# Cross attention over 257 keys: chunks of 128 + 128 + 1 in place of three chunks of 86

## The reference

```
qh = (q @ Wq.T).reshape(B, Tq, H, hd).transpose(0, 2, 1, 3)
kh = (k @ Wk.T).reshape(B, Tk, H, hd).transpose(0, 2, 1, 3)
vh = (v @ Wv.T).reshape(B, Tk, H, hd).transpose(0, 2, 1, 3)
...
scores = jnp.einsum('bhqd,bhkd->bhqk', qh, kh) / np.sqrt(hd)
scores = scores + attn_mask
scores = jnp.where(key_padding_mask[:, None, None, :], NEG_INF, scores)
attn = jax.nn.softmax(scores, axis=-1)
out = jnp.einsum('bhqk,bhkd->bhqd', attn, vh)
...
return out @ Wo.T
```

## Time and profile before

| | |
|---|---|
| time, median of 3 runs (lowest to highest) | 2710.31 us (2709.35 to 2710.75) |
| profiled execution | 2713.56 us |
| its span, first to last instruction | 2711.9 us |
| mean granted TensorE clock | 0.925 |
| busy share of the span: PE, PEld, DVE, ACT, POOL | 84%, 63%, 62%, 50%, 41% |
| the loop of this stage, PE busy in 600 us of it | 595.87 us |
| the same, DVE, ACT, POOL | 465.06, 426.63, 331.55 us |

### The profile page before, as it was taken

One profiled execution on the slowest core, in us unless ns is written; L12 is line 12 of the kernel. 1 busy time (PEld: TensorE's weight loads), 2 busy tenths in 40 slices (PEclk: granted clock), 3 DMA queues, 4 the chain that ended last, 5 costly groups with the idle time before them and its releaser, 6 DMA issues. The chain is left out here.

```text
span 2711.9 us, 91330 instructions
## 1 busy us (share of the span) xinstructions
PE 2288.5 (84%) x32292; PEld 1709.6 (63%) x32293; DVE 1673.4 (62%) x4691; ACT 1360.2 (50%) x3761; POOL 1123.8 (41%) x1094
## 2 busy tenths in 40 slices
PE   6968888883999949996999999999788888649990
PEld 3646666662788736774777777777555555536670
DVE  3556666665677653333777777777578888643341
ACT  2544444442677523332777777777555556412330
POOL 0013333331677510003555555555166666475114
PEclk9989999995999759997999999999899999859995
DMA  4610000000000000001111001100000000022112
GB/s 125 175 46 1 0 0 0 0 0 3 2 0 0 1 28 5 0 0 37 32 30 39 29 29 35 34 29 29 29 2 0 0 0 0 1 96 80 37 37 66
DMA packets 34605, 71.67 MB, mean 26 GB/s; under 512 B 6864, under 2 KB 22224, under 8 KB 33744
## 3 DMA queue, kind: packets, MB, share of 16 engines
q1 hardware_dynamic: 29904, 60.99, 7.6%
q0 software_dynamic: 4608, 9.45, 1.1%
HBM read 60.98 MB, written 9.44 MB: 26 GB/s over the span
## 5 line engine op out<-in xcount | busy, mean ns | idle before, releaser
L2529 DVE CUSTOM_DVE_ANT_0 xat_scores<-bank,xat_mask_b 128x257 f32<-128x257 f32 x512 | 212.8, 423 | 100.9 <-PE bank L2247 92.2
L2401 ACT ACTIVATE xat_scores<-xat_scores,xat_least 128x257 f32<-128x257 f32 x512 | 257.4, 503 | 15.0 <-DVE xat_least L2529 14.9
L2304 PE MATMUL bank<-ident,xat_scores 128*86 128x128 f32 x1536 | 241.0, 280 | 0.0
L2304 PEld LDWEIGHTS bank<-ident,xat_scores 128*86 128x86 f32 x1536 | 158.0, 122 | 83.5 <-ACT xat_scores L2401 40.9
L989 POOL TENSOR_TENSOR gqa_rnorm<-gqa_norm_min,gqa_minus_half 128x12 f32<-128x12 f32 x64 | 145.8, 2278 | 126.7 <-DVE gqa_norm_min L1058 126.7
L2415 ACT ACTIVATE xat_p_T<-bank 86x384 f32<-86x384 f32 x256 | 122.6, 479 | 121.9 <-PE bank L2304 121.9
L624 POOL TENSOR_TENSOR lin_k_exp<-lin_k_exp,lin_k_rsum 128x512 f32<-128x512 f32 x64 | 67.0, 1047 | 266.4 <-DVE lin_k_rsum L662 261.8
L1707 DVE SCALAR_TENSOR_TENSOR X<-bank,expert_shares,X 128x128 f32 (+1 forms) x256 | 72.2, 344 | 156.6 <-PE bank L1670 156.4
L1399 POOL TENSOR_TENSOR bat_scores<-bat_scores,bat_max 128x512 f32<-128x512 f32 x128 | 131.7, 1040 | 56.0 <-DVE bat_max L1432 55.0
L1693 ACT ACTIVATE moe_gelu<-bank 128x512 f32<-128x512 f32 x128 | 76.4, 597 | 153.5 <-PE bank L1662 153.5
L1670 PEld LDWEIGHTS bank<-moe_w,moe_gelu 128*128 128x128 f32 x1024 | 124.2, 192 | 30.1 <-issue 18.7
(11 more groups left out here) (301 smaller groups left out, 6359.7 us busy)
## 6 DMA issues: line engine op xcount, KB each, us to landing
glu_ctx_N<-in_ctxN SPq DMA_DIRECT2D x32, 576.0 KB, 4.4
xat_ctx_T<-in_ctxT SPq DMA_DIRECT2D x32, 516.0 KB, 3.5
expert_w<-in_glx_w SPq DMA_DIRECT2D x3, 2048.0 KB, 15.7
xat_pad<-in_xat_pad SPq DMA_DIRECT2D x32, 128.5 KB, 3.4
slot_rows<-glx_zero POOLq DMA_DIRECT2D x40, 64.0 KB, 10.5
slt_rows<-slot_rows SPq DMA_DIRECT2D x40, 64.0 KB, 1.8
slot_results<-slt_y POOLq DMA_DIRECT2D x40, 64.0 KB, 1.8
moe_w<-in_moe_w SPq DMA_DIRECT2D x2, 1024.0 KB, 5.8
```

What stands on the lines that cost most here:

```text
L2304: m = pe.transpose(dst[0:JC, c * P:(c + 1) * P], sx[j % 2][g][:, c * JC:(c + 1) * JC], k.ident[:, :])
L2401: act.activation(sx[j % 2][g][:, 0:J], sx[j % 2][g][:, 0:J], ACT.Exp, bias=mn[j % 2][g][:, 0:1], scale=-1.0, accum_out=sm[j % 2][:, g:g + ...
L2529: dve.tensor_tensor_reduce(sx[j % 2][g][:, 0:J], pS[g][:, 0:J], mb[slot][:, j, :], 1.0, BIG, ALU.add, ALU.min, mn[j % 2][g][:, 0:1]).then_ ...
```

## The change

`v` and the turned exponentials are kept with 128 keys on the partitions for each of the first two chunks. The last key (number 256) is handled apart, in small products:

- `p_transpose`: two transposes of 128 x 128 for each group in place of three of 128 x 86. With group 3, four products (form 128*32) of the last score column, repeated 32 times, with the identity bring the last key of each of the four groups into 32 partitions of the same bank; the copy of group 3 is 384 columns wide as before, those of groups 0 to 2 are 256 wide.
- `v`: two products of 128 keys in place of three of 86, and four products of 32 columns (form 128*32, 32 moving columns) for the last key. Its copy is 288 columns in place of 384.
- `o`: eight products with 128 rows in place of twelve with 86, and four with one active row, at partitions 0, 32, 64 and 96, for the last key, added to the same results.

No wait, no order of the parts and no other function is changed.

```diff
+    FULL = J // P
+    LAST = J - 1
+    width = [FULL * P] * (G - 1) + [FULL * P + P]
...
-        va = [sb(f"v{i}", [JC, NJ, P]) for i in range(2)]
+        va = [sb(f"v{i}", [P, 2 * P + 32]) for i in range(2)]
...
-        pt = [[sb(f"p_T{i}_{g}", [JC, NJ * P]) for g in range(G)] for i in range(2)]
+        pt = [[sb(f"p_T{i}_{g}", [P, width[g]]) for g in range(G)] for i in range(2)]
...
-                for c in range(NJ):
+                for c in range(FULL):
                     for g in range(G):
                         r = slice(32 * g, 32 * g + 32)
-                        m = pe.matmul(dst[r, OC], va[j % 2][:, c, r], pt[j % 2][g][:, c * P:(c + 1) * P],
-                                      start=(c == 0), stop=(c == NJ - 1))
+                        pe.matmul(dst[r, OC], va[j % 2][:, c * P + 32 * g:c * P + 32 * g + 32],
+                                  pt[j % 2][g][:, c * P:(c + 1) * P], start=(c == 0), stop=False)
+                for g in range(G):
+                    one_row = slice(32 * g, 32 * g + 1)
+                    m = pe.matmul(dst[32 * g:32 * g + 32, OC], va[j % 2][one_row, FULL * P:FULL * P + 32],
+                                  pt[j % 2][G - 1][one_row, FULL * P:FULL * P + P], start=False, stop=True)
                 m.then_inc(no_made, 1)
...
-                for c in range(NJ):
-                    m = pe.matmul(dst[0:JC, c * P:(c + 1) * P], cT[slot][:, j, c * JC:(c + 1) * JC], wv[:, :],
+                for c in range(FULL):
+                    pe.matmul(dst[:, c * P:(c + 1) * P], cT[slot][:, j, c * P:(c + 1) * P], wv[:, :],
+                              start=True, stop=True)
+                for g in range(G):
+                    m = pe.matmul(dst[32 * g:32 * g + 32, FULL * P:FULL * P + 32],
+                                  cT[slot][:, j, LAST:LAST + 1].broadcast_to([P, 32]), wv[:, 32 * g:32 * g + 32],
                                   start=True, stop=True)
...
-                for c in range(NJ):
-                    m = pe.transpose(dst[0:JC, c * P:(c + 1) * P], sx[j % 2][g][:, c * JC:(c + 1) * JC], k.ident[:, :])
+                for c in range(FULL):
+                    m = pe.transpose(dst[:, c * P:(c + 1) * P], sx[j % 2][g][:, c * P:(c + 1) * P], k.ident[:, :])
+                if g == G - 1:
+                    for i in range(G):
+                        m = pe.matmul(dst[32 * i:32 * i + 32, FULL * P:FULL * P + P],
+                                      sx[j % 2][i][:, LAST:LAST + 1].broadcast_to([P, 32]), k.ident[:, :],
+                                      start=True, stop=True)
...
-                act.activation(va[j % 2][:, :, :], unit_bank(*at)[0:JC, 0:NJ * P].rearrange("p (c f) -> p c f", f=P),
-                               ACT.Copy).then_inc(v_copied, 1)
+                act.activation(va[j % 2][:, :], unit_bank(*at)[:, 0:FULL * P + 32], ACT.Copy).then_inc(v_copied, 1)
...
-                act.activation(pt[j % 2][g][:, :], unit_bank(*at)[0:JC, 0:NJ * P], ACT.Copy).then_inc(pa_copied, 1)
+                act.activation(pt[j % 2][g][:, :], unit_bank(*at)[:, 0:width[g]], ACT.Copy).then_inc(pa_copied, 1)
...
-                dve.tensor_copy(pt[j % 2][g][:, :], unit_bank(*at)[0:JC, 0:NJ * P]).then_inc(pd_copied, 1)
+                dve.tensor_copy(pt[j % 2][g][:, :], unit_bank(*at)[:, 0:width[g]]).then_inc(pd_copied, 1)
```

## The result

| | before | changed |
|---|---|---|
| median of 4 runs (lowest to highest) | 2710.53 us (2709.35 to 2714.51) | 2753.39 us (2746.52 to 2763.76) |
| profiled execution | 2713.56 us | 2757.49 us |
| its span | 2711.9 us | 2755.7 us |

The changed kernel is slower: ratio 1.0159, 95% interval 1.0122 to 1.0196, or +43 us in the medians and +44 us in the profiled executions. The forecast was 2748 us, 1.4% slower, with a range of 2729 to 2760. A second set of runs of both gave 1.0172 (1.0135 to 1.0209).

What follows compares the result with a forecast made beforehand. TensorE's own program was taken as the bound. Fewer full records against more changes of form gave +0.36 us a step, +46 us for 128 steps, less 8 us of waits: +38, so 2748 us, 1.4% slower, range 2729 to 2760.

Steps and rivals of the forecast that it cites:

- TensorE's own program is the bound: In the loop TensorE is busy 595.87 of 600 us, with a small wait in some steps.
- Fewer full records: Transposes of groups 0 and 1 lose two records, -0.20 us a step; group 2 loses one, -0.11.
- The change inside `o`: In `o`, the new change from 32 columns x 128 rows to 32 x 32: +0.15 us a step.
- Group 3: Group 3's transposes with the last key's small products: from 0.36 to 0.73 us, +0.37 a step.
- `v` and what follows it: `v`'s full and small products and the next group's new start: mean +0.17 us a step.
- The sum: All terms of a step together: +0.38 us, taken as 0.36, or +46 us for 128 steps.
- The waits of step 0 and 1: TensorE's waits before the scores, 0.18 us in step j = 0 and 0.06 in j = 1, go: -8 us.
- Copies cost and bring nothing: Shorter copies on VectorE and ScalarE only lengthen their idle time as long as TensorE is the bound.
- no price inside `o`: Rival: the change from 128-row to 32 x 32 form in `o` is free, 19 us less, 2729 us; 8%.
- only with a wait: Rival: a change of form costs only where TensorE also waits for a semaphore; 2705 us, 0.2% faster; 5%.
- products of one row don't share the array: Rival: `o`'s four one-row products run one behind the other, +0.65 us a step, 2832 us; 3%.
- Free changes, faster: Rival: changes of form overlap with the records around them; if free, -46 us, 2664 us; 4%.

Runs made afterwards that it cites:

- keep_later: `last_behind_o` with VectorE's `o_keep` moved behind `least` of group 3: 2728.92 us, 0.9944 of the kernel before.
- o_all_rows: Changed kernel with `o`'s four last-key products taking all 128 rows instead of one (output not the reference's): 2737.31 us, 18 us under the changed kernel.
- v_last_first: Changed kernel with `v`'s four small products put ahead of its two full ones: 2719.28 us, 1.0048 of the kernel before.
- spread_apart: Kernel before with the four products spreading the reciprocals moved out of `o`, between keys and group 2's transposes: 2776.00 us, 1.0120 of the kernel before.
- last_behind_o: Changed kernel with the last key's small products of group 3 and `v` both directly behind `o`: 2695.77 us, 0.9957 of the kernel before.

## Why the prediction was right, and what was mis-sized

The direction, the mechanism and the time held; 38 us were forecast, 43 to 44 measured. The 5 us between are one term that was too small and a rounding the wrong way, less smaller errors against them. The terms hold one by one, group by group of the table; only in the last few us is the nearness owed to errors that cancel.

- *TensorE's own program is the bound.* Right before, and more so after: 599.98 of 600 us.
- *Fewer full records.* -0.20 and -0.11 forecast, -0.21 and -0.11 read.
- *The change inside `o`*, bounded by nothing and 0.15 and taken as 0.15: 0.13, shown by the all-rows kernel.
- *Group 3*: +0.37 forecast and read.
- *`v` and what follows it*: the term that was too small. I had 0.055 us for the slow start of full products with 128 weight columns, from L809. That is a transpose, one pass. `v`, the queries and the output projection are two-pass products (two records each), and after a change they start 0.10 late: the output projection has 1.09 - 0.98 = 0.11 more. `v` itself has the 0.05 too, in every step, but its small products were priced 0.02 too dear, so the table shows less. In the mean of the four steps the term is 0.22 us where I had 0.17, 6 us in 128 steps.
- *The sum*: worked out it was 0.38, and I took 0.36. That rounding added 2 to 3 us to the shortfall. `o`'s 0.15 for 0.13 took about as much back. The steps grew by 0.07, 0.40, 0.47 and 0.46 us, and with the 0.24 of waiting that went, TensorE's own work grew by 1.64 / 4 = 0.41 a step: 52 us, less the 8 of the waits 44.
- *The waits of step 0 and 1*, 8 us, vanish: step j = 0 grew from 4.96 to 5.03 us in the mean, against 0.47 and 0.46 in j = 2 and 3. The trace's list of waits has none of TensorE for `least` any more, where the earlier trace rows had 54. Right, and `keep_later` shows the chain at work, in the kernel with both sets behind `o`.
- *Copies cost and bring nothing*: VectorE's copy of 256 columns takes 414 ns for 546, ScalarE's 374 for 479, and all of it went into idle time.

Of the rivals, "no price inside `o`" falls by the timeline and by `o_all_rows`; "only with a wait" by `v_last_first`, where moving products that had no wait ahead of them gave 36 us; "products of one row don't share the array" by the timeline after, where eight one-row records take 0.35 us to the next group and eight 128-row records 0.36; the clock stayed at 1.00. "Free changes, faster" was wrong in its premise, and of its 46 us (1.7%) the best order that keeps the output gives 0.44%: two of the new changes stand in it still. The rule of the Trainium skill, TensorEngine Tiling (Array Packing), section Key Properties, that a change of tiling mode drains the engine, agrees with `spread_apart`: 0.27 us for two changes. The overhead of about 60 cycles a matmul that the same page of the Trainium skill gives (section Instruction Overhead) does not fit here if it is charged to each record in turn: by the prediction's estimate from it `v`'s eight small records would take 0.2 us by themselves. They take 0.19 us with the change behind them, of which from the first start to the last 0.07.

What stays open: the whole-program time of one kernel differs by up to 1.4% between chips (2705 to 2744 us) while its steps in this loop don't. The traces show where, not why. In `last_behind_o` the products of L1887, in a later stage, stretch over 83 us on the one chip and 115 on the other, and there the profile lists waits of ScalarE and VectorE for "remote" (36.5 and 26.1 us) that the trace of the shorter one lacks; the other traces agree with the trace of their chip. The first stage differs too, 116 to 127 us, even between traces of one chip, with code that is the same in all kernels. Both lie outside the change.

## What to carry to other kernels

Where TensorE is the bound, count the changes between full products, column groups and row groups as work: in this loop two of them cost as much as two and a half records of 128 columns. A small remainder is cheap if its products stand beside others of the same form, and dear where they stand between full ones; one and the same set of products was 1.6% slower or 0.4% faster than the kernel before by its place in the order alone. And when a term's price is taken from a neighbour, take one with the same weight load, not only with the same columns.

## What the runs showed of the hardware

The slow start of a group follows the length of its first weight load. The list of weight loads of the changed kernel in its loop, mean ns behind the busy time:

```profile
L2315 PEld LDWEIGHTS bank<-ident,xat_scores 128*128 128x128 f32 x869 | 98.2, 141 | 68.7 <-ACT xat_scores L2416 34.5 <-issue 23.2
L2285 PEld LDWEIGHTS bank<-xat_w_v,xat_ctx_T 128*128 128x128 f32 x432 | 56.3, 190 | 21.5 <-issue 21.5
L2318 PEld LDWEIGHTS bank<-ident,xat_scores 128*32 128x32 f32 x872 | 17.0, 107 | 18.3 <-issue 18.3
```

A load of 107 ns goes with a start that is 0.02 us late, 141 ns (128 columns of a transpose) with 0.055, 190 ns (128 columns of a two-pass product) with 0.10: in each case the load's length less some 0.085 us. Where one form follows the same form without a wait, the start isn't late: the loads overlap the products ahead. It fits that `v`'s group of four is 0.61 us long where it stands behind transposes, in `last_behind_o`, and 0.71 where it stands behind small rounds, in `v_last_first`.

The late start doesn't need a change of form, though. In the kernel without the last key `v` stands behind transposes and is 0.71 us long as well, because TensorE waited there for a copy and the load couldn't start earlier (1613.72 in that timeline). So a change of form costs two things that can be told apart: some 0.09 us between the groups, which a wait that is met in time doesn't cost, and the part of the first weight load that no longer hides, which a wait can cost too. The rule of load length less 0.085 us is a reading of four groups (the fourth is the turned groups of the kernel before, 122 ns and 0.04), not a separate experiment.
